# State-space stage: the head products of two steps are made together in every odd step

## The reference

```python
proj = input_states @ in_proj_w.T                     # gate, x, B, C, dt
xBC = silu(conv(xBC) + conv_b)                        # 4 taps along the tokens, per channel
scores = einsum('bcihn,bcjhn->bcijh', Cc, Bc) * Ldec * dtc
y_intra = einsum('bcijh,bcjhp->bcihp', scores, xc)
states = einsum('bcjh,bcjhn,bcjhp->bchpn', dtc * dlast, Bc, xc)   # then a scan over the chunks
y_inter = einsum('bcihn,bchpn->bcihp', Cc * exp(cum), prev)
y = (y_intra + y_inter) + D * x
g = y * silu(gate);  g = (g * rsqrt(mean(g * g, per group of 1024) + eps)) * norm_w
out = g @ out_w.T
```

## The kernel before

| step | 0 | 1 | 2 | 3 | 4 | 5 | 6 | 7 | 8 | 9 | 10 | 11 | 12 | 13 | 14 | 15 |
|---|---|---|---|---|---|---|---|---|---|---|---|---|---|---|---|---|
| entry | x4 | g4 | x5, g5 | x6 | g6 | x7, g7 | B | C | g0 | x0 | x1 | g1 | x2 | x3 | g2, turn B | g3, products |

## Time and profile before

### The profile page before, as it was taken

The page is one execution under the profiler, slowest core; times in us unless marked ns, Lnnn a source line. Parts: engine busy times, 40 slices in busy tenths (PEclk is TensorE's granted clock), DMA queues, the critical chain, the costliest instruction groups (busy, mean ns, idle before and its releaser), DMA issues.

```text
span 2086.4 us, 33789 instructions
## 1 busy us (share of the span) xinstructions
PE 2057.9 (99%) x12040; PEld 1550.7 (74%) x12040; DVE 1466.8 (70%) x1815; ACT 1335.4 (64%) x2376; POOL 868.3 (42%) x758
## 2 busy tenths in 40 slices
PE   7999999999999999999999999999999999999999
PEld 6655554688877777877777777777777777888887
DVE  4566666486678878778688787787787786555556
ACT  4255555536678788787887887878778783232332
POOL 1011111130357657667566675666666672000000
PEclk9999999999999999999999999999999999999999
DMA  5523222243545454544545555455455467554452
GB/s 185 169 59 86 76 74 56 86 136 95 158 147 179 146 166 158 168 147 164 169 151 159 162 162 158 153 158 172 145 173 163 149 209 256 149 151 142 145 187 86
DMA packets 182782, 305.35 MB, mean 146 GB/s; under 512 B 20416, under 2 KB 96704, under 8 KB 182496
## 3 DMA queue, kind: packets, MB, share of 16 engines
q1 hardware_dynamic: 182624, 303.29, 46.5%
HBM read 249.90 MB, written 53.06 MB: 145 GB/s over the span
## 4 chain that ended last, share of the span: by engine, by line
PE 90%; DVE 5%; ACT 2%; POOL 1%; issue 1%; DMA 1%; SPq 0%; DVEq 0%; POOLq 0%; ACTq 0%
PE ssm_pp L156 16%; PE ssm_pp L158 15%; PE ssm_pp L157 15%; PE att_gu L686 6%; PE ssm_py L1478 5%; PE ssm_py L1473 4%; PE ssm_pstate L1457 4%; DVE stk_mx L351 3%; PE ssm_turn L1434 2%; PE att_rows L341 2%; PE ssm_py L156 1%; PE ssm_py L158 1%; PE ssm_py L157 1%; PE down_ps L156 1%; PE down_ps L158 1%; PE down_ps L157 1%
## 5 line engine op out<-in xcount | busy, mean ns | idle before, releaser
L156 PE MATMUL ssm_pp<-xhi,ssm_lo 128*128 128x512 f32 x1192 | 478.8, 402 | 0.9 <-DVE ssm_bc L1720 0.4
L158 PE MATMUL ssm_pp<-xhi,ssm_hi 128*128 128x512 f32 x1192 | 465.5, 391 | 0.0
L157 PE MATMUL ssm_pp<-xlo,ssm_hi 128*128 128x512 f32 x1192 | 464.9, 390 | 0.0
L1605 ACT ACTIVATE ssm_sct<-ssm_cumb,ssm_gpar 128x128 f32<-128x128 f32 x1024 | 313.0, 390 | 55.5 <-PE ssm_py L1478 49.4
L148 POOL TENSOR_TENSOR ssm_lo<-ssm_raw,ssm_hi 128x512 fp32r<-128x512 f32 x146 | 238.8, 1641 | 77.8 <-ACT ssm_hi L137 77.8
L156 PEld LDWEIGHTS ssm_pp<-xhi,ssm_lo 128*128 128x128 f32 x1192 | 223.6, 188 | 63.6 <-issue 19.0
L1720 DVE SCALAR_TENSOR_TENSOR ssm_xc<-ssm_pp,vectors,ssm_xc 128x1022 f32<-128x1022 f32 (+2 forms) x192 | 245.2, 1277 | 23.6 <-ACT ssm_xc L1559 18.9
L158 PEld LDWEIGHTS ssm_pp<-xhi,ssm_hi 128*128 128x128 f32 x1192 | 223.8, 188 | 48.1
L157 PEld LDWEIGHTS ssm_pp<-xlo,ssm_hi 128*128 128x128 f32 x1192 | 224.0, 188 | 42.6
L1755 DVE TENSOR_TENSOR ssm_sct<-ssm_sct,ssm_cbm 128x1024 f32<-128x1024 f32 x128 | 229.3, 1792 | 26.5 <-ACT ssm_sct L1612 26.5
L1908 POOL TENSOR_TENSOR ssm_go<-ssm_t,ssm_gt 128x512 f32<-128x512 f32 x128 | 167.3, 1307 | 169.2 <-DVE ssm_t L1791 169.2
(11 more groups left out here) (288 smaller groups left out, 4135.1 us busy)
## 6 DMA issues: line engine op xcount, KB each, us to landing
ssm_cumb<-dt_sums SPq DMA_DIRECT2D x96, 1024.0 KB, 5.7
ssm_raw<-w SPq DMA_DIRECT2D x150, 256.0 KB, 3.7
gated<-ssm_go SPq DMA_DIRECT2D x128, 256.0 KB, 2.6
ssm_cumb<-dt_sums SPq DMA_DIRECT2D x32, 512.0 KB, 4.0
ssm_gt<-w SPq DMA_DIRECT2D x64, 256.0 KB, 2.7
ssm_xc<-gated SPq DMA_DIRECT2D x32, 512.0 KB, 4.2
ssm_sct<-gated SPq DMA_DIRECT2D x32, 512.0 KB, 4.3
ffn_raw<-w SPq DMA_DIRECT2D x37, 256.0 KB, 2.8
```

What stands on the lines that cost most here:

```text
L156: pe.matmul(out, wlo, xhi, start=start, stop=False)
L157: pe.matmul(out, whi, xlo, start=False, stop=False)
L158: return pe.matmul(out, whi, xhi, start=False, stop=stop)
L1605: i = act.activation(sct[:, s % 2, h, :], cumb[:, s % 2, 0, h, :], ACT.Relu, scale=-1.0, bias=gpar[:, unit, 0, s % NTOK, h:h + 1])
```

## The change

TensorE leaves the head products out of even steps and makes those of two steps, s-1 and s, one block behind the other, in every odd step, after its turns and its state product. The other engines follow: VectorE finishes both steps at the start of the next even step, ahead of growth and scores; GpSimd gates step s-2 instead of s-1 and adds the squares of s-3 instead of s-2, and its decay stands ahead of the gating in even steps and behind it in odd ones; SyncE stores s-2. ScalarE's order stays. No instruction is added or left out, and no buffer or semaphore.

```diff
@@ sync @@
-                    if before(g, s, 1):
-                        write(*before(g, s, 1))
+                    if before(g, s, 2):
+                        write(*before(g, s, 2))
...
+            write(G - 1, NS - 2)
             write(G - 1, NS - 1)
@@ tensor, in scan(g, s) @@
                     squares(unit)
+
+            def outputs(g, s):
+                ch = s % NC
                 pe.wait_ge(xp_done, g * NS + (s + 1))
                 pe.wait_ge(st_done, g * NS + (s + 1))
                 after(pe, t2_done, g * NS + (s - 1))
...
                     scan(g, s)
+                    if s % 2 == 1:
+                        outputs(g, s - 1)
+                        outputs(g, s)
                     for e in at(s, last)[1:]:
                         entry(g, e)
@@ vector @@
                         advance(*before(g, s, 1))
+                    if s % 2 == 0 and before(g, s, 2):
+                        finish(*before(g, s, 2))
+                        finish(*before(g, s, 1))
                     grown(g, s)
                     scores(g, s)
-                    if before(g, s, 1):
-                        finish(*before(g, s, 1))
...
+            finish(G - 1, NS - 2)
             finish(G - 1, NS - 1)
@@ gpsimd @@
-                    decay(g, s)
-                    if before(g, s, 1):
-                        output(*before(g, s, 1))
-                    ahead = last and s >= HALF_AT
-                    if ahead and behind(g, s, 1, last):
-                        weigh(*behind(g, s, 1, last))
+                    if before(g, s, 3):
+                        add_squares(*before(g, s, 3))
+                    if s % 2 == 0:
+                        decay(g, s)
                     if before(g, s, 2):
-                        add_squares(*before(g, s, 2))
-                    if not ahead and behind(g, s, 1, last):
+                        output(*before(g, s, 2))
+                    if s % 2 == 1:
+                        decay(g, s)
+                    if behind(g, s, 1, last):
                         weigh(*behind(g, s, 1, last))
             passes(pool, body)
+            add_squares(G - 1, NS - 3)
+            output(G - 1, NS - 2)
             output(G - 1, NS - 1)
```

## The result

The changed kernel takes **2293.74 us** (median of 4 runs, 2291.9 to 2294.77) against 2086.67 us (4 runs) for the kernel before: 1.0994 of the time, 95% interval 1.0979 to 1.1009. Slower was right, 2237 us was 57 us too little, and the time lies 4 us above the range.

A forecast was written before the change was run, and what follows sets the result against it. TensorE, busy 99% of the span, was taken to bound the kernel. Joins -16, stalls +139, the end +1 and clock +26 gave +150 on 2087.34, forecast 2237 us, range 2175 to 2290.

The forecast's parts named there:

- x6, step 3: TensorE's weight tile x6 in step 3 waits for VectorE's convolution of x5: 2.76 us a group.
- x7, step 5: TensorE's weight tile x7 in step 5 waits for VectorE's convolution, ready at 11.04, due at 8.56: 2.48 us.
- B, step 6: TensorE's weight tile B in step 6 waits for VectorE's convolution of x7: 3.08 us.
- x0, step 9: TensorE's weight tile x0 in step 9 waits for VectorE's convolution, with no table load in the chain: 1.16 us.
- g1, step 11: TensorE's weight tile g1 in step 11 waits for VectorE's convolution, ready at 11.04, due at 8.56: 2.48 us.
- g2, step 14: TensorE's weight tile g2 in step 14 waits for VectorE's convolution of x2: 2.06 us.
- turn of B, step 14: TensorE's turn of B in step 14 waits for VectorE's convolution of x3, behind an unbroken VectorE queue: 4.13 us.
- L: The end of the even step's head products in a joined block, from which ready and due times are counted.
- GpSimd's gating and squares, one step later: GpSimd's delayed gating and squares cost nothing: they wait for finishing, and their next reader is a step away.
- The clock: TensorE's granted clock falls after two of six gaps a group, 1.7 us each: +26 us; none 0, all +75.
- the clock falls at every gap: Rival: TensorE's clock falls behind every gap, 75 us in all, giving 2286 us; chance 0.10.
- The joins: TensorE's joined head blocks save 0.25 us per pair of steps, 64 pairs: -16 us, bounds -9 and -23.

The follow-up runs named there:

- two_buffers: tuned2 with two ssm_sct buffers again, all its moves of convolutions, gating, decay and squares kept: 2112.64 us (kernel before: 2086.19).
- tuned2: Changed kernel plus third ssm_sct buffer, paired gating and squares, odd-step entries' convolutions moved earlier (x3's to step 14), GpSimd's decay and ScalarE's squares forward: 2070.99 us.
- gate_pair: Changed kernel, but GpSimd gates both steps of a pair in the even step, right after their finishing: 2240.32 us.
- fill2: Changed kernel with unread matmuls ahead of waiting tiles, those of step 6 and the turn of B writing to other banks, none ahead of g2: 2250.9 us.
- tuned2_again: The kernel tuned2 once more, timed five times beside nine executions of the kernel before: 2070.48 us against 2086.19, ratio 0.9921.
- fill: Changed kernel with unread matmuls put ahead of the weight tiles that wait, at six places a group: 2276.75 us (kernel before: 2084.5).

## Why the prediction was right and where it failed

**The direction and the mechanism: right.** The lags reuse the buffer of the products two steps back; the join moves these from a step ahead to 1.8 us ahead; lags, Exp, mask product and convolution follow, and the tile two entries on waits. The list of waits shows just that (323 us of lags waiting, 122 of tiles), and `two_buffers` and `tuned2` show it from the other side.

**The places.** Start to start, in the group shown above:

| place | forecast | measured |
|---|---|---|
| x6, step 3 | 2.76 | 3.10 |
| x7, step 5 | 2.48 | 2.49 |
| B, step 6 | 3.08 | 3.20 |
| x0, step 9 | 1.16 | 1.33 |
| **g1, step 11** | **2.48** | **7.45** |
| scores, steps 12 and 13 | 0.1 | 0 |
| g2, step 14 | 2.06 | 1.67 |
| turn of B, step 14 | 4.13 | 3.02 |
| g3, step 15 | none | 0.51 |
| sum | 18.25 | 22.8 |

Seven of the nine are within 0.7 us, one is 1.1 too large. The hits at x7 and g1 (in `gate_pair`) are in part luck. By the forecast the convolution ends 11.04 us after L (its terms add up to 11.02) and the tile is due at 8.56; in the trace x7 starts 10.63 after L and was due at 8.14, since the state product holds up the next tile by only 0.46 us and that tile's second product by the rest. Both terms were 0.4 too late, and their difference came out. Two small things balance over a group: x7, x0 and g1, once they wait, take 5.6 instead of 5.87 us, and the 0.51 of g3 is 1.17 in five groups of seven. That each chain starts anew from a joined block, so that they add, holds. The step that failed is "GpSimd's gating and squares, one step later": costed at nothing, it makes ScalarE wait 7.53 us in step 9, 5.0 us of which reach TensorE, in each group. `gate_pair` took away just those. Over the run, waits came to some 170 us up to the middle of the last group, where 139 were forecast for the whole; 35 us of it are this place.

**The clock: the term that was mis-sized.** 26 us were taken (a fall behind two of six gaps, 1.7 us each); the products behind gaps ran over by 51 us. A fall was about the right size behind x6 and B, 1.6 us, and too small behind g1 and the turn of B, whose tiles take 7.0 to 8.4 us (1.4 to 2.8 too much). The number was too low: of seven groups, the tiles of x6 and B were slow 9 times out of 14, that of g1 and that behind the turn of B 7 times out of 7 each, so 23 against the 15 that were taken. The rival "the clock falls at every gap" (2286 us, 0.10) came within 8 us of the time, but by luck: it has 75 us of clock and 139 of waits, one too large and the other too small; x7, whose gap is 2.5 us start to start, had one fall in seven. What the Trainium skill says (TensorE: Matmul & The Clock Gate, HAM oscillation), that a wait throttles TensorE and the next burst starts cold, the trace bears out in part. At g1 it holds in all seven groups: the clock was at its lower level 2.0 to 4.3 us before the tile began. Behind gaps of 3 us it does not hold as stated: 5 of 14 tiles were not slowed at all, and in 8 of the 9 slow ones the clock fell only 0.4 to 1.5 us after the tile had begun. Where `fill2` kept TensorE busy, it was 1.00 over both tiles shown.

**The joins: a little better than taken.** 0.25 us a pair was the sum, 0.33 is what `tuned2` shows without any wait: -21 instead of -16 us, within the bounds of -9 to -23. The joined blocks gave 0.16 for 0.14; the state product and the tile behind it 0.20 (0.46 + 5.87 us, where they took 0.95 + 5.58) for 0.11, in seven of a group's eight pairs (behind the state product of step 14 stands the turn of B).

**The sum.** -21 + 170 + 51 = 200 us; the other 7 of the 206.7 us between the spans lie in the rest of the last group, where TensorE waits 1.65 us for xp, 3.41 for a copy of sums of squares and 1.20 ahead of head products. Each of these terms is good to some 5 us: against `tuned2_again`, which has the same order on TensorE and no wait in seven groups, the changed kernel is 205 us longer in those seven, 161 of them waits and 44 clock, and with the last group the clock comes to 47 and the rest of that group to 11. Against +150 on record that is 31 more for the waits (35 at g1, 4 less elsewhere), 25 more for the clock, 5 less by the joins, and some 6 in the last group. The range had room for one of the two misses and not for both together; that the clock's loss grows with every missed wait was not in it either.

## What to carry to other kernels

When a step is moved later, ask of each of its buffers not only who reads the result but who writes next into what the step reads; here the writer was a silu on a third engine, and its wait cost 35 us of the 207, more than all that the change saved (21). Work that TensorE makes in larger pieces moves every reader's start by the piece: count the buffers first, then move the readers, then join; with a third buffer, a gating right behind its input, no convolution behind a late one and decay and squares moved forward, the kernel with the same join, which had lost 10%, gains 0.8%. And price a gap of TensorE with the products behind it: here a gap of 3 us had another 1.6 us behind it in 9 cases of 14, and one of 6.9 us always 1.4 to 2.8.

## What was not expected of the hardware

The same gap does not always bring the clock down. These tiles waited 2.96 to 3.04 us in the changed kernel, at two places of the group:

```profile
760.39 0.50 PE L156 MATMUL ssm_pp<-xhi,ssm_lo 128*128 128x512 f32 x1 [2.96 <-DVE ssm_xc L1727]
...
798.62 0.50 PE L156 MATMUL ssm_pp<-xhi,ssm_lo 128*128 128x512 f32 x1 [3.04 <-DVE ssm_xc L1727]
...
936.37 0.50 PE L156 MATMUL ssm_pp<-xhi,ssm_lo 128*128 128x512 f32 x1 [2.96 <-DVE ssm_xc L1727]
```

The first two took 5.60 and 5.58 us, the third 7.18 (from each start to that of the turns behind). Of the 14 gaps at these two places in seven groups (2.93 to 3.05 us, the first 2.55), 9 had a slow tile behind them and 5 had not; of the seven gaps of 6.9 us all had one, of the seven of 1.9 us one. That is why the groups of the changed kernel differ (174.7 to 179.3 us) with the same waits in them. What decides it in a single case no row here shows.

Fillers must be ready when the gap begins. Ten of them, in `fill` at step 6, started 3.64 us into the gap and took 4.63 us instead of 2.3, since the granted clock was 0.50 from their first to their last: they cost more than the fall that they were to prevent (1.6).
